# A recommender tower on one core: one tile shape for all matmuls, the last top layers in pieces, the first loads on two DMA queues

## The reference

```
e  = stack([tbl_m[ids[:, m]] for m in range(32)], axis=1)      # (1024, 32, 16)
x0 = xk = e
for W in (W0, W1, W2):                                         # (32, 32 or 64, 64)
    xk = relu(einsum('bmd,bhd,mhk->bkd', x0, xk, W))           # (1024, 64, 16)
    outs.append(sum(xk, axis=2))
h = concatenate([outs, dense_ctx], axis=1)                     # (1024, 192 + 16)
h = relu(h @ W_top1 + b_top1)                                  # 512
h = relu(h @ W_top2 + b_top2)                                  # 256
y = h @ W_top3                                                 # 1
```

## Time and profile before

| | us |
|---|---|
| median of 3 runs | 656.53 (656.3 to 657.41) |
| the profiled execution | 655.24 |
| its span | 653.3 |
| TensorE matmuls busy | 586.3 (90%) |
| VectorE busy | 545.9 (84%) |
| GpSimd busy | 513.9 (79%) |
| ScalarE busy | 353.2 (54%) |

### The profile page before, as it was taken

The page is one execution under the profiler, slowest core; times in us unless marked ns, Lnnn a source line. Parts: engine busy times, 40 slices in busy tenths (PEclk is TensorE's granted clock), DMA queues, the critical chain, the costliest instruction groups (busy, mean ns, idle before and its releaser), DMA issues.

```text
span 653.3 us, 7670 instructions
## 1 busy us (share of the span) xinstructions
PE 586.3 (90%) x2692; PEld 200.6 (31%) x2692; DVE 545.9 (84%) x345; ACT 353.2 (54%) x540; POOL 513.9 (79%) x373
## 2 busy tenths in 40 slices
PE   0027789899999799999999999999999999999998
PEld 0002223232333233332343324332333333333434
DVE  0002989899998799999999999999999998999780
ACT  0002574455756447555666666555755576666541
POOL 6777769388889888988898888888888876568650
PEclk9999799999999799999999999999999999999999
DMA  8649999950189917994499639990899249950000
GB/s 256 174 54 250 253 177 238 271 159 4 17 179 234 244 32 134 236 233 97 66 248 234 154 29 218 233 222 8 166 224 248 59 81 255 219 133 0 1 2 0
DMA packets 88438, 98.67 MB, mean 151 GB/s; under 512 B 59880, under 2 KB 66416, under 8 KB 88384
## 3 DMA queue, kind: packets, MB, share of 16 engines
q1 hardware_dynamic: 76064, 90.11, 60.4%
q0 software_dynamic: 8192, 2.11, 3.2%
q10 hardware_dynamic: 4144, 5.96, 2.8%
HBM read 95.01 MB, written 7.61 MB: 157 GB/s over the span
## 4 chain that ended last, share of the span: by engine, by line
PE 69%; DVE 6%; DMA 5%; ACT 5%; issue 2%; DVEq 0%; ACTq 0%
PE acc L470 61%; DVE z L692 6%; DMA x0rep<-x_rows 5%; ACT xk L560 3%; PE top L425 2%; PE acc L466 2%; PE top L417 1%; PE top L418 1%; PE xk L409 1%; ACT xk_copy L571 1%; PE top L432 1%; ACT xk L535 0%; ACT squares L521 0%; ACT xk L553 0%; DVEq L688 0%
## 5 line engine op out<-in xcount | busy, mean ns | idle before, releaser
L692 DVE TENSOR_TENSOR z<-xk,x0rep 128x2048 f32<-128x2048 f32 (+1 forms) x295 | 520.1, 1821 | 55.2 <-DMA x0rep<-x_rows 26.9
L470 PE MATMUL acc<-z,w_sb 128*64 128x512 f32 x1852 | 439.6, 605 | 20.3 <-DVE z L692 20.0
L401 POOL TENSOR_TENSOR z_pool<-x0rep,xk_copy 128x1024 f32<-128x1024 f32 x113 | 268.6, 2379 | 49.6 <-PE acc L470 32.2
L355 POOL DMA_INDIRECT emb<-tbl,idx x256 | 245.1, 957 | 68.6 <-issue 62.4
L470 PEld LDWEIGHTS acc<-z,w_sb 128*64 128x64 f32 x1852 | 128.4, 138 | 298.9 <-issue 225.3
L560 ACT ACTIVATE xk<-xk_copy 32x1024 f32<-32x1024 f32 x128 | 130.5, 1019 | 102.7 <-DVE z L692 101.4
L470 PE MATMUL acc<-z_pool,w_sb 128*64 128x512 f32 x452 | 116.4, 593 | 0.0
L571 ACT ACTIVATE xk_copy<-acc 64x512 f32<-64x512 f32 x128 | 75.5, 590 | 8.7 <-PE acc L470 7.6
L553 ACT ACTIVATE xk<-lay 128x1024 f32<-128x1024 f32 x16 | 16.4, 1028 | 78.3 <-DVE z L692 62.4
L409 PE MATMUL acc<-w_sb 128*64 128x512 f32 x24 | 12.4, 665 | 44.1 <-DMA emb<-tbl,idx 44.1
L470 PEld LDWEIGHTS acc<-z_pool,w_sb 128*64 128x64 f32 x452 | 32.1, 137 | 63.1 <-issue 60.8
(11 more groups left out here) (19 smaller groups left out, 97.6 us busy)
## 6 DMA issues: line engine op xcount, KB each, us to landing
x0rep<-x_rows SPq DMA_DIRECT2D x128, 512.0 KB, 16.0
lay<-x_rows SPq DMA_DIRECT2D x32, 512.0 KB, 9.9
emb<-tbl,idx POOLq DMA_INDIRECT x256, 2.4
w_long<-w ACTq DMA_DIRECT2D x4, 768.0 KB, 6.9
squares<-x_rows SPq DMA_DIRECT2D x16, 128.0 KB
x_rows<-emb SPq DMA_DIRECT2D x7, 256.0 KB, 4.6
x_rows<-emb SPq DMA_DIRECT2D x9, 128.0 KB, 6.1
w_sb<-w_long ACTq DMA_DIRECT2D x8, 128.0 KB
```

The costliest lines, as they stand in the source:

```text
L355: pool.indirect_dma_start(out=emb[:, i % 2, m, :], out_offset=None, in_=tables[m], in_offset=bass.IndirectOffsetOnAxis(ap=idx[:, i, m:m + ...
L401: pool.tensor_mul(z_pool[:, (count - 1) % POOL_RING, :], x0rep[:, g % X0_GROUPS, slot, :], xk_copy[:, side, :]).then_inc(z_pool_ready, 1)
L470: mm = pe.matmul(bank[c * H:(c + 1) * H, :], w[:, tile, :], src[:, c * COLS:(c + 1) * COLS], start=(k == 0), stop=last)
L692: dve.tensor_mul(z[:, at:at + wide, :], both, src).then_inc(z_ready, wide)
```

## The change

Four things are changed together.

1. All matmuls inside the loop use weights of 64 columns on 128 rows of the array (80 for the third part of `make_h1`, as before). `squares` gets 128 partitions and a buffer of its own per side, `w0d_sb` 128 rows; both are cleared by VectorE at the start (two more memsets), so the square matmuls contract over 128 rows of which 96 are zero. Its load is one DMA and not two, and it waits for the clearing. `make_h1`, `make_h2` and `keep_busy` issue two matmuls of 64 weight columns for each one of 128 (or, in `keep_busy`, alternate halves). `make_y` takes h2 as weights and `wt3` as the moving operand, one column: the result stands as 128x1, so `take_y` and the output's DMA go over 128 partitions.
2. The top layers of the last tile are written out anew (`make_last`): the first part of h1 starts before the last sum is there, the last evacuation and the last sum are done in two halves, ScalarE and VectorE share the bias and relu pieces, each m or k has a PSUM bank and a semaphore of its own, and one `keep_busy(1)` is left of six.
3. The loads of tile 0, side A: ScalarE's DMA queue issues `x0rep` 0, the second `lay`, and `x0rep` 3, 5, 7; SyncE's queue the first `lay`, `x0rep` 1, 2, `squares`, `x0rep` 4, 6.
4. `N_TOP_LOADS` goes from 8 to 7, since one DMA of `w0d` is gone.

```diff
@@ squares and w0d
-        w0d_sb = sb("w0d_sb", [SIDES * M, H])
+        w0d_sb = sb("w0d_sb", [P, H])
-        squares = sb("squares", [SIDES * M, WIDE])
+        squares = sb("squares", [P, SIDES, WIDE])
...
+            dve.memset(w0d_sb[:], 0.0)
+            dve.memset(squares[:], 0.0).then_inc(cleared, 1)
...
-                            pe.matmul(bank[c * H:(c + 1) * H, :], w0d_sb[side * M:(side + 1) * M, :],
-                                      squares[side * M:(side + 1) * M, c * COLS:(c + 1) * COLS],
+                            pe.matmul(bank[c * H:(c + 1) * H, :], w0d_sb[:],
+                                      squares[:, side, c * COLS:(c + 1) * COLS],
@@ top layers in the loop
-                    o = top[:, m * P:(m + 1) * P]
-                    pe.matmul(o, wt1_sb[:, 0, m * P:(m + 1) * P], in12[:], start=True, stop=False)
-                    last = pe.matmul(o, wt1_sb[0:K3, 1, m * P:(m + 1) * P], in3[:], start=False, stop=True)
+                    for half in range(2):
+                        pe.matmul(top[halves[half], m * P:(m + 1) * P], wt1_sb[:, 0, columns_of(m, half)],
+                                  in12[:], start=True, stop=False)
+                    for half in range(2):
+                        last = pe.matmul(top[halves[half], m * P:(m + 1) * P], wt1_sb[0:K3, 1, columns_of(m, half)],
+                                         in3[:], start=False, stop=True)
...
-                    last = pe.matmul(top[0:1, 0:P], wt3_sb[:, k:k + 1], h2[:, k, :],
-                                     start=(k == 0), stop=(k == F2 // P - 1))
+                    for half in range(2):
+                        last = pe.matmul(top[halves[half], 0:1], h2[:, k, halves[half]], wt3_sb[:, k:k + 1],
+                                         start=(k == 0), stop=(k == F2 // P - 1))
@@ first loads, SyncE and then ScalarE
-            load_side(0, A)
+            load_lay(sp, 0, A, 0)
+            for slot in (1, 2):
+                load_x0(sp, 0, A, slot)
+            load_rows(sp, 0, A)
+            for slot in (4, 6):
+                load_x0(sp, 0, A, slot)
             load_side(0, Bs)
...
+            for g in range(len(FIRST_GROUPS)):
+                act.wait_ge(saved_first[g], 32 if g == 0 else 16)
+            load_x0(act, 0, A, 0)
+            load_lay(act, 0, A, 1)
+            for slot in (3, 5, 7):
+                load_x0(act, 0, A, slot)
@@ the last tile's top layers, TensorE
-            keep_busy(4, xk[:, 0, 0:COLS])
-            make_h1(NT - 1)
-            keep_busy(2, xk[:, 0, 0:COLS])
-            make_h2(NT - 1)
-            make_y(NT - 1)
+            make_last()
+            def make_last():
+                pe.wait_ge(last_in12, 1)
+                for m in range(F1 // P):
+                    for half in range(2):
+                        pe.matmul(h1_bank[m][halves[half], :], wt1_sb[:, 0, columns_of(m, half)], in12[:],
+                                  start=True, stop=False)
+                keep_busy(1, top)
+                pe.wait_ge(last_in3_act, 1)
+                pe.wait_ge(last_in3_dve, 1)
...
+                    op.then_inc(last_h1_made, 1)
...
+                        pe.wait_ge(last_h1_act, k // 2 + 1)
...
+                        pe.wait_ge(last_h1_dve, k // 2 + 1)
...
+                pe.wait_ge(last_h2_act, 1)
+                pe.matmul(top[0:1, 0:P], wt3_sb[:, 0:1], h2[:, 0, :], start=True, stop=False)
+                pe.wait_ge(last_h2_dve, 1)
+                pe.matmul(top[0:1, 0:P], wt3_sb[:, 1:2], h2[:, 1, :], start=False, stop=True).then_inc(last_y_made, 1)
@@ the last evacuation and sum, ScalarE and VectorE
+            for n in range(2):
+                cols = slice(n * COLS // 2, (n + 1) * COLS // 2)
+                act.activation(layer_out[:, taken % OUTS, cols], bank[:, cols], ACT.Relu).then_inc(last_out, 1)
...
+            for half in range(2):
+                dve.wait_ge(last_out, half + 1)
...
+                dve.tensor_reduce(sums[:, half * ROWS // 2:(half + 1) * ROWS // 2],
+                                  rows.rearrange("p (b d) -> p b d", d=D), AX_X, ALU.add).then_inc(last_summed, 1)
```

More of the change, by code:

```diff
@@ L244, in copied_before, with columns, load_lay, load_rows @@
             return sum(PHASES[m][1] < 2 for m in range(n + 1))
+        def columns(i, side):
+            return (i * SIDES + side) * WIDE
+        def load_lay(queue, i, side, n):
+            src = bass.AP(x0_rows, E_SHIFT[n] * PITCH + columns(i, side),
+                          [[2 * PITCH, GROUPS], [2 * PITCH, PER_GROUP], [1, WIDE]])
+            queue.dma_start(lay[:, side, n, :], src).then_inc(lay_in[side][n], 16)
+        def load_rows(queue, i, side):
+            if i == 0:
+                queue.wait_ge(cleared, 1)
+            queue.dma_start(squares[0:M, side, :],
+                         bass.AP(x0_rows, columns(i, side), [[PITCH, M], [1, WIDE]])).then_inc(rows_in[side], 16)
+        def load_x0(queue, i, side, slot):
+            g = (i * SIDES + side) % X0_GROUPS
+            src = bass.AP(x0_rows, slot * PITCH + columns(i, side),
+                          [[2 * PITCH, GROUPS], [0, PER_GROUP], [1, WIDE]])
+            queue.dma_start(x0rep[:, g, slot, :], src).then_inc(x0_in[g][slot], 16)
         @block.sync
@@ L275, in save_x0 @@
                 sp.dma_start(dst, emb[:, i % 2, lo:hi, :]).then_inc(done, 16)
[L277 to L296, removed]
             def load_side(i, side):
@@ L424, in make_h2 @@
                     for k in range(F1 // P):
-                        last = pe.matmul(top[:, m * P:(m + 1) * P], wt2_sb[:, k, m * P:(m + 1) * P],
-                                         h1[:, k, :], start=(k == 0), stop=(k == F1 // P - 1))
+                        for half in range(2):
+                            last = pe.matmul(top[halves[half], m * P:(m + 1) * P], wt2_sb[:, k, columns_of(m, half)],
+                                             h1[:, k, :], start=(k == 0), stop=(k == F1 // P - 1))
                 last.then_inc(unit_ready, 1)
@@ L591, in inputs @@
                     op.then_inc(inputs_in, 1)
+                elif row == rows[-1]:
+                    op.then_inc(last_in12, 1)
             def take_h1(i):
@@ L610, in take_y @@
                     act.wait_ge(y_out, 16 * i)
[L611 removed]
+                act.activation(y_sb[:], top[:, 0:1], ACT.Copy).then_inc(unit_taken, 1)
             taken = 0
@@ L694, in _ @@
                         sum_over_d(phase)
-            sum_over_d(PHASES[-1])
+            n = len(PHASES) - 1
+            sums = row_sums[:, (NT - 1) % 2, len(SUM_ROWS) - 1, :]
+            for half in range(2):
+                dve.wait_ge(last_out, half + 1)
+                rows = layer_out[:, n % OUTS, half * COLS // 2:(half + 1) * COLS // 2]
+                dve.tensor_reduce(sums[:, half * ROWS // 2:(half + 1) * ROWS // 2],
+                                  rows.rearrange("p (b d) -> p b d", d=D), AX_X, ALU.add).then_inc(last_summed, 1)
+            dve.wait_ge(last_summed, 2)
+            dve.tensor_copy(in3[0:H, LAST_IN3 + ROWS:LAST_IN3 + 2 * ROWS], sums[H:P, :]).then_inc(last_in3_dve, 1)
+            for m in range(1, F1 // P, 2):
+                dve.wait_ge(last_h1_made, m + 1)
+                dve.tensor_scalar(h1[:, m, :], xk[:, m // 2, COLS:COLS + P], bt1_sb[:, m:m + 1], 0.0, ALU.add, ALU.max
+                                  ).then_inc(last_h1_dve, 1)
+            dve.wait_ge(last_h2_made, 2)
+            dve.tensor_scalar(h2[:, 1, :], acc[:, (len(PHASES) + 1) % ACCS, 0:P], bt2_sb[:, 1:2], 0.0, ALU.add, ALU.max
+                              ).then_inc(last_h2_dve, 1)
 def kernel(**inputs):
```

89 lines of the change are left out of this document (67 added, 22 removed).

## The result

| | before | the change |
|---|---|---|
| median, 8 runs each (us) | 657.02 | 653.27 |
| lowest to highest (us) | 656.3 to 658.7 | 649.74 to 655.95 |
| profiled execution, its time and its span (us) | 655.24, 653.3 | 655.95, 654.0 |

The ratio is 0.9935, 95% interval 0.991 to 0.996: 0.65% less time, about 4 us and clear of noise, where 12.0 were forecast; 653.27 lies outside 640.0 to 650.0. The runs of the change also spread over 6.2 us, those of before over 2.4.

The account below looks back on a forecast made before the run. Loads were taken to bound until 221 us, TensorE and VectorE level until about 530, then TensorE. Start +2.0, middle -4.8, last tiles -2.8, tail -6.3 sum to -11.9, rounded to 12.0 off 656.5: 644.5 us, range 640.0 to 650.0.

Parts of the forecast that it names:

- What bounds the kernel: Up to 221 us waits for loads; to about 530 VectorE's waits for TensorE are the gain; from there TensorE bounds.
- The tile shape: Loop matmuls: changes of shape cost TensorE 0.43 us each for h1 and h2, 0.25 for y, 0.29 a square.
- the rival of the issue bound: Loop's h1 and h2: many short matmuls cost issue time, 0.062 us a record; 648 us, chance 0.10.
- the rival of no overlap: Loop's h1 and h2: short matmuls in alternate halves do not overlap, 3.4 us; slower, 662 us, chance 0.03.
- Start, +2.0: Tile 0's loads: slot 2 ends later with two queues; third product and GpSimd's chain delayed, +2.0 us net.
- two queues bring more bytes: Tile 0's loads: rival that two queues move more bytes, start -2 and not +2; 640.5 us, chance 0.15.
- the bound of −2: Tile 0's start, fast bound: six transfers of 1.4 us in place of five of 2.1.
- Middle and last tiles, −4.8 and −2.8: From 221.49 us, VectorE's waits for TensorE: 1.5, then 3 x 1.1 us; from 531 to 641, TensorE's savings count fully.
- the three signs of being wrong: Third product before 59 us, h1 longer than 2 us, or the last step's end moving less than 3 us.
- Tail, −6.3: Last step's end to y's copy: 4.6 to 4.7 us in place of 10.9; gain bounds 4.8 and 6.8.
- h2's last four matmuls 0.6: Tail: after h1's last bias piece, four matmuls of h2 remain before its bias, 0.6 us.
- the lower bound of 4.8: Tail: gain of only 4.8 us if TensorE's clock is at 1.2 GHz, since `keep_busy` is gone.

Follow-up runs that it names:

- experiment 3: Second kind of chip, column kept: y issued behind side B's loads, ratio 0.9887 to the kernel before; issued from ScalarE's queue instead of SyncE's, 0.9932.
- before_again: The kernel before, unchanged, run again on the first kind of chip for its trace: 657.88 us.
- y_row_again: The change with the loop's y as a row of one partition again, first kind of chip: 647.83 us, ratio 0.9863 to the kernel before.
- experiment 2: First kind of chip: kernel before 657.55 us, change unchanged 654.66, change with y as a row 647.83, kernel before with only the last tile's edits 651.07.
- before_3: The kernel before, unchanged, run again on the second kind of chip for its trace: 693.59 us.

## Why the prediction was wrong

**What bounds the kernel.** Right as far as it went. TensorE is busy 10.9 us less and the span gains nothing by itself; up to 221 us the loads bound it, behind that the two engines. What was missed is that the loads can bind in every tile once something holds them up.

**The tile shape.** Right. h1, TensorE in order of time:

```profile
256.96 1.89 PE L543 MATMUL acc<-z,w_sb 128*64 128x512 f32 x8
258.68 0.39 PE L448 MATMUL top<-in,wt_sb 128*64 128x128 f32 x4
...
260.44 1.03 PE L543 MATMUL acc<-z,w_sb 128*64 128x512 f32 x4
```

1.76 us for 32 records, against 1.71 forecast and 1.99 before; there is no gap on entry (eight records at 0.43 a pair lead from 256.96 to 258.68). y and a square:

```profile
276.78 0.35 PE L469 MATMUL top<-wt_sb,h 128*64 128x1 f32 x8
276.98 1.06 PE L543 MATMUL acc<-z_pool,w_sb 128*64 128x512 f32 x4
277.87 4.46 PE L543 MATMUL acc<-z,w_sb 128*64 128x512 f32 x20
282.16 1.03 PE L539 MATMUL acc<-squares,w0d_sb 128*64 128x512 f32 x4
283.02 2.31 PE L543 MATMUL acc<-z,w_sb 128*64 128x512 f32 x10
```

y takes 0.20 in place of 0.53, the square 0.86 in place of 1.00 and starts on time. 1.76 us for 32 is 0.055 us a record, which puts the rival of the issue bound (0.062, and the 62 ns that the Trainium skill's page TensorE: Matmul & The Clock Gate gives only for hardware decode off) and the rival of no overlap out: h1 would have taken 1.98 or 3.4.

**Start, +2.0.** Right in size, and in mechanism but for one part: +2.35 at the third product, and GpSimd's chain at 129.19 where 128.8 was forecast. The first product was to come 1.1 us later, since the first `lay` was to end together with slot 0; it comes 0.17 later (53.20), so that `lay` was not held up so. That two queues bring more bytes is out: from 54 to 62 us the change moves 245 and 230 GB/s, before 252 and 234. The 1.4 us a transfer that the bound of −2 rested on stands in no run.

**Middle and last tiles, −4.8 and −2.8: the step that failed.** It is the sentence "y as 128x1 in the loop costs TensorE the same four slots, and its DMA has nobody waiting close behind." Its first half holds. The second looked only at who waits for y itself, and not at what is queued behind it: side B's two `lay` and eight `x0rep` follow in the same queue, and experiment 3 shows that even another queue's transfers stall. The working named no price for 128 writes of four bytes; the trace before had the near row for it, one write of 512 bytes that ends in 1.4 us. Measured: 7.4 us for the 128 writes alone, transfers at 81 to 155 GB/s for some 8 us beside them (tile 3 of the two traces), 8.5 us more of waits for loads on one chip (17.1 against 8.6; 9.7 between the first two traces), and 6.8 us of time (5.4 against the first result's median). Without it the two terms come out near their size: from the product that waits at 223.90 in `before_again`'s trace (225.74 in `y_row_again`'s) to the last tile, `y_row_again` goes from 1.8 us behind to 5.0 us ahead, 6.8 of the 7.6. By place these are 2.4 where 1.5 were forecast (to the wait at 276.41 of the earlier trace rows), 2.3 where 3.3 were (the three places behind it), and 2.1 where 2.8 were (the last tiles). A part of the 2.4 may be luck: TensorE had been idle 3.3 to 3.4 us through the wait for tile 2's loads, and its granted clock then averages 0.52 from 224 to 232 us in `before_again` and 0.79 in `y_row_again`. Of the 2.4 us 1.6 are gained in the 12 us behind that wait, and how much of them is the clock's and how much the shape's isn't shown. VectorE's waits for TensorE, which were to fall from 15.5 to under 8, fell to 10.6 in the change and to 10.1 in `y_row_again`. And of the three signs of being wrong one came: the last step's end did not come 3 us earlier but 5.9 later, 646.90 against 640.96, where the prediction had it 5.6 earlier.

**Tail, −6.3.** Right in mechanism, 1.0 too much. The end after, all engines in order of time:

```profile
646.94 0.66 ACT L735 ACTIVATE layer_out<-acc 128x256 f32<-128x256 f32 x2 [5.88 <-PE acc L543]
...
648.46 1.06 PE L488 MATMUL xk<-in,wt_sb 80*64 80x128 f32 x16
...
649.42 1.97 PE L500 MATMUL acc<-h,wt_sb 128*64 128x128 f32 x32
651.21 0.37 ACT L744 ACTIVATE h<-acc,bt_sb 128x128 f32<-128x128 f32 x1 [1.49 <-PE acc L500]
...
652.26 0.27 ACT L747 ACTIVATE y_last<-top 1x128 f32<-1x128 f32 x1 [0.69 <-PE top L507]
```

The first 1.5 us are as worked out: h1's second part starts at 648.46, 1.56 behind the last step's end at 646.90. From there to y's copy it is 4.1 us, not 3.1. The term that was too small is "h2's last four matmuls 0.6": I took the other twelve to be hidden behind h1's biases, but h2 can't start before the first bias piece, it starts at 649.42, and its 16 matmuls (32 records) then take 1.8 us in a row. TensorE is the bound of that stretch, at a granted clock of 1.00; the lower bound of 4.8, which rested on a clock of 1.2 GHz, is therefore not what was seen.

**The number.** With y as a row 12.0 us stand against 9.7 measured on the chip of experiment 2: the tail's 1.0 is part of what is left, and the forecast would still have been too high. Range and chances suffered from the same gap: no rival had the loads as the new wait in the middle, though the change turns y's DMA in front of them into 128 writes.

## What to carry to other kernels

Whoever turns an output to save an engine a fraction of a us should look at what its DMA becomes: y as a column saved TensorE a third of a us a tile and cost the kernel 2 to 7 in all, since 128 writes of four bytes hold up the loads, also those of another queue. Keep small outputs contiguous, or issue them when no load is due. A transfer's price is not only who waits for it, but who is under way beside it. And filler work for an engine is priced like work wherever it keeps the engine's real work from being done before a hold-up, as tile 0 on the second kind of chip shows. Two traces are compared on one chip, and each against its median, before a difference is put down to an edit: the 6.0 us at tile 2 of the first two traces look like y's doing, and between two traces from one chip y's part there is 0.5.

## What was not expected of the hardware

128 writes of four bytes to 512 bytes of DRAM, issued at 697.40, end 7.4 us later where one write of 512 bytes needs 1.4; beside loads the whole traffic drops from some 240 GB/s to 81 and 93 over 4 us each when SyncE's queue, which also holds the loads, issues them, and to 111 and 145 when ScalarE's does.

The same kernel takes 657 us on one kind of chip and 692 on others. On the latter the first product of before starts at 67 us, not 53, and the second phase of tile 0 at 103.8, not 66.6, while the DMA is at a share of 1.05. In `before_3` TensorE ends tile 0's first phase at 78.73, and ScalarE, which waits for that phase alone, starts at 101.42. In between no engine but GpSimd computes or gathers, and from 88 us on not even GpSimd (columns as in rows 2):

```profile
88.00:92.00 4.00, 0.00 (x0) 0.00 (x0) 0.00 (x0) 0.00 (x0) 0.00 (x0) 0.50 1.07 232
```

Where TensorE still has work then, it gets single matmuls 2 to 3 us apart with "issue" as what ended the wait. So it is not TensorE alone that is held up. What the engines waited for the traces don't show, and it wasn't tried.
